# Issuing the setup's loads of x and of the projection weights from ScalarE's DMA queue instead of SyncE's

## The reference, cut to what matters

```
xn = _layernorm(x)
# attention: q = xn @ Wq; for each of 3 heads: k = xn @ Wk[i], v = xn @ Wv[i],
#   scores = (q k^T) * decay ** max(s - t - 1, 0) for s > t, else 0
#   blended += softmax(xn @ Wg)[i] * (scores @ v);  s = blended @ Wo * out_scale
# feed-forward: every weight is one of 16 table values, picked by an index
gate = xn @ lut[gate_idx].T ; up = xn @ lut[up_idx].T      # 512 -> 1376
g = silu((silu(gate) * up) @ lut[down_idx].T)              # 1376 -> 512
out = x + s * g
```

## Time and profile before

| | |
|---|---|
| median of 3 runs | 1794.44 us (1792.72 to 1795.2) |
| the profiled execution's own time | 1792.32 us |
| its span in the trace | 1790.5 us |
| PE busy | 98% of the span |
| DVE, ACT, POOL busy | 79%, 47%, 58% |
| setup, to the first matmul of the main part | 136.4 us |

### The profile page before, as it was taken

The page is one execution under the profiler, slowest core; times in us unless marked ns, Lnnn a source line. Parts: engine busy times, 40 slices in busy tenths (PEclk is TensorE's granted clock), DMA queues, the critical chain, the costliest instruction groups (busy, mean ns, idle before and its releaser), DMA issues.

```text
span 1790.5 us, 44626 instructions
## 1 busy us (share of the span) xinstructions
PE 1758.0 (98%) x17096; PEld 1514.3 (85%) x17096; DVE 1412.7 (79%) x2814; ACT 847.8 (47%) x1494; POOL 1033.1 (58%) x1039
## 2 busy tenths in 40 slices
PE   6999999999999999999999999999999999999998
PEld 2338888898988988898898889898888989899887
DVE  8898878787787878788787878778777878878685
ACT  3785454454545444454544445454534545454443
POOL 9303746656474755647474664747466564747354
PEclk9999999999999999999999999999999999999999
DMA  9976686978768696886868697786859677785853
GB/s 235 336 308 166 175 233 164 260 170 211 223 173 239 171 247 167 232 205 180 239 168 243 167 247 187 201 227 175 236 161 259 169 222 213 171 249 167 216 158 120
DMA packets 411041, 371.09 MB, mean 207 GB/s; under 512 B 222576, under 2 KB 278640, under 8 KB 410752
## 3 DMA queue, kind: packets, MB, share of 16 engines
q1 hardware_dynamic: 399824, 361.36, 73.0%
q0 software_dynamic: 11008, 6.89, 2.5%
HBM read 294.34 MB, written 35.52 MB: 184 GB/s over the span
## 4 chain that ended last, share of the span: by engine, by line
PE 94%; ACT 2%; DMA 1%; POOL 1%; DVE 1%; issue 1%; SPq 0%; POOLq 0%; ACTq 0%; DVEq 0%
PE F L2044 53%; PE F L2098 20%; PE B L2044 6%; PE F L2079 2%; PE B L1950 2%; PE B L1922 2%; PE B L1921 2%; PE B L1920 2%; PE F L1822 2%; POOL codes L772 1%; PE F L1920 1%; PE F L1921 1%; PE F L1922 1%; ACT ring L967 1%; DMA dblocks<-xt 1%
## 5 line engine op out<-in xcount | busy, mean ns | idle before, releaser
L2044 PE MATMUL F<-xtc,ring 128*128 128x256 f16 (+1 forms) x4224 | 497.7, 273 | 0.0
L2044 PEld LDWEIGHTS F<-xtc,ring 128*128 128x128 f16 (+1 forms) x4224 | 416.1, 100 | 42.4
L2098 PE MATMUL F<-ring,region 128*128 128x256 f16 x3360 | 382.5, 273 | 0.0
L2044 PE MATMUL F<-xt,ring 128*128 128x256 f16 (+1 forms) x3168 | 377.2, 273 | 0.0
L2098 PEld LDWEIGHTS F<-ring,region 128*128 128x128 f16 x3360 | 328.0, 98 | 47.8
L2044 PEld LDWEIGHTS F<-xt,ring 128*128 128x128 f16 (+1 forms) x3168 | 310.5, 100 | 31.2
L967 ACT ACTIVATE region<-region 128x512 f16<-128x512 f32 (+4 forms) x288 | 152.4, 529 | 290.4 <-DVE region L1686 116.6
L876 POOL TENSOR_TENSOR region<-hs,region 128x1024 f16<-128x1024 f32 x80 | 175.3, 2192 | 103.6 <-ACT region L967 103.6
L916 POOL TENSOR_TENSOR chalf<-tt,chalf 128x1024 f16<-128x1024 f32 x30 | 63.9, 2129 | 199.3 <-ACT chalf L967 199.3
L967 ACT ACTIVATE region<-F 128x512 f32<-128x512 f32 (+1 forms) x200 | 114.8, 576 | 92.4 <-PE F L2098 45.3
L894 POOL TENSOR_TENSOR x_out<-x_out,region 128x512 f32<-128x512 f32 x62 | 82.2, 1326 | 87.3 <-DVE region L1757 87.3
(11 more groups left out here) (293 smaller groups left out, 3500.4 us busy)
## 6 DMA issues: line engine op xcount, KB each, us to landing
ring<-blocks SPq DMA_DIRECT2D x546, 256.0 KB, 3.2
ring<-dblocks SPq DMA_DIRECT2D x224, 256.0 KB, 3.3
x_next<-in_x SPq DMA_DIRECT2D x64, 256.0 KB, 3.6
x_out<-in_x SPq DMA_DIRECT2D x64, 256.0 KB, 3.2
out_y<-x_out SPq DMA_DIRECT2D x64, 256.0 KB, 5.3
ring<-blocks SPq DMA_DIRECT2D x112, 128.0 KB, 2.5
ring<-dblocks SPq DMA_DIRECT2D x112, 128.0 KB, 2.8
blocks<-ring SPq DMA_DIRECT2D x35, 256.0 KB, 8.4
```

What stands on the lines that cost most here:

```text
L2044: ins = T_.matmul(out_, a, b, start=fresh, stop=False, skip_group_check=True)
L2098: ins = T_.matmul(bank[:, j * HV:(j + 1) * HV], a, b, start=fresh, stop=False, skip_group_check=True)
```

## The change

The four DMAs of each load of x, and the nine DMAs of the weights, are issued by ACT instead of SP. ACT issues them in its own loop behind `store(b)` and ahead of `x_high` and of the unit's sums. The places in the tables change with it: x at unit 1 (SP: 7), the second x at unit 21 (SP: 26), the weights at units 5, 6, 8 and 9 (SP: 12 to 15). As SP's loop is about six units ahead of the other engines, these are about the same moments. The wait for `s_xh` in front of the second x moves to ACT too. SP keeps its own `load_x` for the main part. Nothing else is changed.

```diff
-        X_AT = 7
-        X2_AT, NORM2_AT = 26, 30
-        WEIGHTS_AT = {12: 0, 13: 1, 14: 2, 15: 3}
+        X_AT = 1
+        X2_AT, NORM2_AT = 21, 30
+        WEIGHTS_AT = {5: 0, 6: 1, 8: 2, 9: 3}
...
@@ SP's loop @@
                 if b < NU:
                     load_codes(b)
-                if b == X_AT:
-                    load_x(row_group(0, 0))
-                if b == X2_AT:
-                    sp.wait_ge(s_xh, GT)
-                    load_x(row_group(0, 1))
-                if b in WEIGHTS_AT:
-                    load_weights(WEIGHTS_AT[b])
                 for s, op in WRITES.get(b, ()):
...
@@ ACT's functions @@
+            def load_x(rows):
+                for t in DOWN:
+                    nc.scalar.dma_start(x_next[:, t], x_v[rows][:, t]).then_inc(s_xn, 16)
+
+            def load_weights(n):
+
+                if n == 0:
+                    nc.scalar.dma_start(a32[:, :, 0:D], wq.rearrange("(c p) d -> p c d", p=P)).then_inc(s_w, 16)
+                    nc.scalar.dma_start(a32[:, :, CGT:QKV], wg.rearrange("(c p) d -> p c d", p=P)).then_inc(s_w, 16)
+                    nc.scalar.dma_start(wo32[:, :], wo).then_inc(s_wo, 16)
+                else:
+                    h = n - 1
+                    nc.scalar.dma_start(a32[:, :, CK + h * D:CK + (h + 1) * D],
+                                 wk[h].rearrange("(c p) d -> p c d", p=P)).then_inc(s_w, 16)
+                    nc.scalar.dma_start(a32[:, :, CV + h * D:CV + (h + 1) * D],
+                                 wv[h].rearrange("(c p) d -> p c d", p=P)).then_inc(s_w, 16)
...
@@ ACT's loop @@
                 if b < NU:
                     store(b)
+                if b == X_AT:
+                    load_x(row_group(0, 0))
+                if b == X2_AT:
+                    act.wait_ge(s_xh, GT)
+                    load_x(row_group(0, 1))
+                if b in WEIGHTS_AT:
+                    load_weights(WEIGHTS_AT[b])
                 if b in XHAT_AT:
```

More of the change, by code:

```diff
@@ L606, in load_x @@
                     sp.dma_start(x_next[:, t], x_v[rows][:, t]).then_inc(s_xn, 16)
[L608 to L619, removed]
             def transpose(dst, src, done):
```

## The result

The changed kernel takes 1801.92 us (median of 6 runs, 1799.38 to 1804.24), the kernel before 1794.82 us: a ratio of 1.0038, 95% interval [1.0028, 1.0048]. It is slower by about 7 us; the forecast was 1794.1 with a range up to 1799. The profiled execution took 1799.38 us with a span of 1797.5, which is 7.0 us more than before.

A forecast was written before the change was run, and what follows sets the result against it. The main part was taken as bound by PE, so only its start at 136.40 us could move. Terms -3.6 + 1.7 + 0.4 + 1.2 = -0.3 us gave 1792.0 us profiled, 1794.1 as median, range 1789.5 to 1799.

The forecast's parts named there:

- part 3: ACT issuing 17 DMAs in the setup: no cost at units 1, 5, 6, 8; +0.4 us at unit 9, +1.2 at 21.
- The dear queue on ACT: Rival: an issue on ACT costs 1.3 us and more as its queue fills: +4.4 us, 1798.8 us; chance 0.13.
- The stall for `dblocks<-xt`: ACT's setup wait for this write, until 73.14 us, goes because SP issues it earlier, near 54 us: -3.6 us.
- x in front of unit 5's codes: In the setup, x issued earlier delays DVE's units 5 to 8: +1.7 us (bounds -1.35 to +3.3).
- The second x at unit 21: Four issues on ACT behind unit 21's copy, ahead of sums PE waits for: +1.2 us (0.6 to 4.7).
- the trade: Likeliest case: the 3.6 us stall goes, about as much is paid for early x and ACT's issues: 1794.1 us; chance 0.64.

The follow-up runs named there:

- wide rows: Changed kernel with the four weight loads of units 8 and 9 replaced by loads of 2 KB rows, leaving out two heads' weights: 1792.87 us, ratio 0.9994.
- x on SP and the weights spread: Changed kernel with both x loads on SP at 7 and 26, weights on ACT at units 5, 8, 10 and 12: 1790.25 us, ratio 0.9981.
- only the last portion later: Changed kernel with the last weights (third head's wk and wv) issued at ACT's unit 12 instead of 9: 1792.51 us, ratio 0.9988.

## Why the prediction was wrong

The 7.06 us add up from the copies of ACT compared above: +1.6 up to unit 9, +4.0 at unit 10, +3.2 to unit 11 (60.81, against 52.01 before), -2.9 from there to unit 16 (79.55 against 73.63), +1.2 at unit 22.

- **The step that failed is in part 3: the price of the weights' issues on ACT, "At unit 9: two issues of 0.6 us ... +0.4 us (0 to 2.0)".** It was 4.0 us, and 3.2 us more followed from it by the clock. I had the row that showed it: `in_wo` on SP took 5.32 us, and I said myself that SP couldn't hand over more while too much was in flight. But I bounded ACT's price by spreading these 5.32 us over four issues. A stall doesn't spread evenly; it fell on one issue (5.32 us on SP, 5.72 us on ACT with x on SP) or on the two of unit 9, and the bound for unit 9 had to be at least the 5.32 us of that row. I also took the weights at units 5, 6 and 8 as covered by the idle time before unit 9, and didn't ask what they leave in flight for unit 9. Those of unit 8 had been issued 4 us before and take 13.5 us (`wk`) and 16.8 us (`wv`) to land, so they were still in flight; with wide rows there are fewer packets of them, and no stall.
- **A term was missing: the clock.** A stall of ACT stops PE, the granted clock falls to 0.50 and the next lookup takes 3.19 us instead of 1.91. +3.2 us on the path, of which keeping PE busy took 2.9 us away. The trace of before has such a stretch too, from 42 us on (the lookup of 3.50 us above), and I left it out of the sum.
- **The dear queue on ACT** was a rival, with the right mechanism, but with most of its price at the wrong place (4.7 us at unit 21, 1.6 at unit 9), so its 1798.8 still fell short; I gave it a chance of 0.13.
- **The stall for `dblocks<-xt`**: it goes, and the issue at 53.72 us is as forecast at 54. That is luck: I took the comparison of unit 11 to end at about 52 us, but it is unit 12's that does. Unit 11's ends at 49.3 in the kernel before. In the changed kernel the comparisons are 2.6 us late, which made up for it. With x on SP and the weights spread, unit 17's codes go out at 49.37 us and the write at 51.07. The landing isn't as forecast. I kept 9.85 us for it and expected 64 us; it took 16.6 us in the changed kernel and 19.5 us with the weights spread. On ACT the gain was 2.9 us instead of 3.6. In the changed kernel ACT doesn't wait for the write at all, as it gets there only at 78.17 us; with the first x at unit 3 it gets there earlier, and waits 2.80 us. Here the sentence of the Trainium skill that I weighed and set aside ("DMA: Bandwidth & Descriptors", "Issuing engines are not separate DMA queues": all run on the same 16 engines and interleave) was half right: the issue came 9.5 us earlier, but the landing only 2.7 (53.72 + 16.6 against 63.20 + 9.9). The DMA engines' share was 1.22 while it was under way, against 1.06 before. That this load is the reason, and not what stands ahead in SP's queue, wasn't tested.
- **x in front of unit 5's codes**: forecast +1.7; unit 5 was 4.1 us late, beyond my bound of 3.3, but at unit 9 it was +1.6 on ACT. A size met by luck: DVE's wait of 1.35 us for unit 8's codes went, DVE was still 2.6 us late at unit 9, and PE's lookup there took 1.0 us less than before (2.50 against 3.50), at a granted clock of 1.00 instead of 0.51 to 0.64, a term that the sum didn't have.
- **The second x at unit 21**: forecast +1.2, measured +1.24, and 1.4 us less between the same copies when undone. Without the stall and the clock the measured terms are +1.6, -2.9 and +1.2, in sum -0.1 against the forecast -0.3, and the run with only the last portion later starts its main part at 136.38 us, against 136.40 before. So the trade was right but for the stall at unit 9 and the clock behind it; these two made the prediction wrong.

What remains open: what makes the queue refuse an issue, and why the medians of the variants lie 1 to 3 us lower against before than the main part's start in their profiles. Part of it is that the two profiled executions of before, 1792.32 and 1791.77 us, are among its fast ones, while most variants' profiles lie within 1 us of their medians.

## What to carry to other kernels

A DMA issue is cheap for a compute engine only while its queue takes it at once. Look at the packets in flight there (short rows are dear: 512 packets for 256 KB here), and price a queue that doesn't as one whole stall, here of 4 to 6 us, on the instruction behind it. Then look whether that place has idle time and what PE's clock does after it. Two issues three units later took 7 us off. And with the DMA engines as full as here, a write issued 9.5 and 12.1 us earlier landed only 2.7 and 2.5 us earlier.

## What the hardware showed that I had not expected

- An issue on ACT costs 0.37 to 0.6 us when its queue has room and runs beside the copy before it (both start at 47.33); the copies behind it wait.
- Loads of 256 KB in rows of 512 B at units 8 and 9 leave ACT idle for 3.9 to 4.6 us at unit 9; nearly the same bytes in rows of 2 KB leave it idle for none.
- Sixty-four useless matmuls, 3.75 us long in PE's idle time, took 2.9 us off the stretch behind them (3.89 against 6.76 us between two copies), as PE kept its clock.
- Five loads that one run hands over in 2.9 us stall for 5.72 us at the fifth in another.
